# Softmax probabilities transposed in 32x32 blocks on VectorE and reordered through DRAM, in an attention and router kernel

## The chip, the cores and the metric

The kernel runs on one core of one Trainium2 chip. The metric is the device time of one execution in microseconds (us). Before the change it is 1690.57 us, the median of 3 runs (1690.31 to 1691.97).

## What is computed

One transformer layer on x of 4 x 512 rows by 512 columns: attention with 32 query heads of 128 and 8 key and value heads, then a router layer over 64 experts. The part that matters here:

```python
h = _layernorm(x) * (1 + ca) + sa
q = (h @ Wq.T).reshape(bsz, q_len, 32, 128).transpose(0, 2, 1, 3)      # then rotary embedding
scores = jnp.einsum('bhqd,bhkd->bhqk', q, k) * scale
scores = jnp.where(causal, scores, -1e9)
attn = jax.nn.softmax(scores, axis=-1)
out = jnp.einsum('bhqk,bhkd->bhqd', attn, v)
x = x + ga * (out.transpose(0, 2, 1, 3).reshape(bsz, q_len, 4096) @ Wo.T)
```

The router layer (layer norm, logits, softmax, the 8 largest, a mix of expert biases) follows for each of 16 tiles of 128 rows.

## The kernel before

A step t handles one query head of one batch row; there are 128 steps (`ALL`). Four steps are a unit u, the four query heads that share one key and value head for one batch row; h = t mod 4 says which. Every product is taken in three passes over operands split in a rounded high part (`_hi`) and the rest (`_lo`), so a transposed probability tile is written twice, as `PT_hi` by ScalarE and as `PT_lo` by VectorE.

Each engine has its own program, written out by hand in `step(t)`, and works it off strictly in order; the engines meet at semaphores. What TensorE does in step t of the old kernel, in this order:

- `transpose_part(t, 0)` and `(t, 1)` (L394): the probabilities of step t, 128x128 tiles, into the banks ta and tb. With part 2 there are 10 tiles, the causal half of 512 x 512 (`CAUSAL` = 1280 columns on 128 partitions).
- `scores(t+1)` (L376), with `transpose_part(t, 2)` in its middle.
- `q_proj(t+3)` (L336), the query projection for three steps on.
- by h: `out_proj(u-1)` at h = 0 (L428, four tiles of 12 matmuls), `k_proj` at h = 1 (L347), `v_proj` at h = 2 (L357), `v_transpose` at h = 3 (L364).
- `values(t)` (L408), probabilities times v, 12 matmuls into the bank pv.

VectorE in step t: `split_part_lo` (L956), `mask_and_max(t+1)` in two halves (L941, L945), `o_split_lo(t-1)` (L962), `invert_sums(t+1)` (L951), `q_rope(t+3)` (L920 to L922), at h = 1 `k_rope` (L927 to L929), at h = 0 `v_split_lo` (L933) and the four `add_out` (L970). ScalarE: `split_part_hi` (L696), `o_split_hi(t-1)` (L700), at h = 2 `k_nope` (L664, L665) and `k_split` (L671), `q_split(t+2)` (L654), `exponentials(t+1)` (L683), `normalise(t+1)` (L690). GpSimd (POOL): `q_split` (L1274), `q_rope` (L1269), `k_rope` (L1278), `k_split` (L1282) and the low parts of the next weights (L1265). SyncE's queue (SP) carries the weight pieces, the rows of x and the results; it has nothing per step.

From step 117 on the router layer runs in the same steps (`ffn_...`), mostly on VectorE and GpSimd.

## Time and profile before

| | |
|---|---|
| median of 3 runs | 1690.57 us |
| the profiled execution | 1689.32 us |
| its span, first to last instruction | 1688.0 us |
| granted TensorE clock, mean | 0.992 |
| busy share of the span: PE, PEld, DVE, ACT, POOL | 98%, 83%, 70%, 60%, 38% |
| chain that ended last, by engine | PE 87%, DVE 7%, issue 3%, ACT 2%, DMA 1%, POOL 1% |
| DMA | 54.20 MB, mean 32 GB/s |

The table is read from the top down: PE busy for nearly the whole span says little by itself, since matmuls overlap; that the chain which ended last lies on PE for 87% says that PE's order of work sets the time. The shares are averages over a prologue of about 100 us, the 117 plain steps and the last steps with the router layer.

### The profile page before, as it was taken

The page shows a single profiled execution, that of the slowest core. Times are in us where ns is not written, and L with a number is a line of the kernel's source. Part 1 is how long each engine was busy: PE and PEld are TensorE (multiplying, and loading weights), DVE is VectorE, ACT ScalarE, POOL GpSimd, SP SyncE. Part 2 cuts the span into 40 slices and gives each one's busy share as a digit, 9 for nine tenths or more (in the row PEclk, how much of TensorE's full clock was granted, in tenths as well). Part 3 has the DMA queues.
Part 4 walks back from the last instruction along what each step waited for, and adds up shares of the span by engine and source line. Part 5 has one row for each costly group of instructions (what it writes and reads, how often), then busy time and mean ns, then how long its engine had stood idle before and what let it go on. Part 6 is the DMA issues. An engine that isn't in the chain of part 4 may idle for free.

```text
span 1688.0 us, 25563 instructions
## 1 busy us (share of the span) xinstructions
PE 1648.9 (98%) x8880; PEld 1401.1 (83%) x8880; DVE 1177.1 (70%) x3413; ACT 1011.1 (60%) x2522; POOL 644.8 (38%) x524
## 2 busy tenths in 40 slices
PE   8999999999999999999999999999999999999977
PEld 5688888888888888888888888888888888887754
DVE  6866667766666667766666667766666667778798
ACT  3366666766656666766656666756656666755441
POOL 2753243423333233423333233423333233455674
PEclk9999999999999999999999999999999999999998
DMA  8410000100000000100000000100000000211032
GB/s 306 158 44 13 1 26 14 26 1 13 26 14 13 1 26 14 26 1 14 26 13 13 1 26 14 26 1 13 26 13 14 1 26 13 65 25 51 26 82 74
DMA packets 48975, 54.20 MB, mean 32 GB/s; under 512 B 19456, under 2 KB 27904, under 8 KB 48848
## 3 DMA queue, kind: packets, MB, share of 16 engines
q1 hardware_dynamic: 48528, 52.47, 10.2%
q8 instruction: 71, 1.16, 0.3%
q14 instruction: 56, 0.46, 0.1%
q10 hardware_dynamic: 320, 0.11, 0.0%
HBM read 45.20 MB, written 7.37 MB: 31 GB/s over the span
## 4 chain that ended last, share of the span: by engine, by line
PE 87%; DVE 7%; issue 3%; ACT 2%; DMA 1%; POOL 1%; SPq 0%; DVEq 0%; ACTq 0%
PE bank_q L336 20%; PE bank_pv L408 14%; PE bank_s L376 13%; PE bank_pv L428 10%; PE bank_x L428 10%; PE bank_x L357 5%; PE bank_ta L394 5%; PE bank_x L347 5%; PE bank_tb L394 3%; PE bank_s L324 1%; DVE PT_lo L956 1%; PE bank_x L364 1%; DMA wmod<-in_wmod 1%; DVE neg_max L945 1%; ACT probs L683 1%
## 5 line engine op out<-in xcount | busy, mean ns | idle before, releaser
L696 ACT ACTIVATE PT_hi<-bank_ta 128x512 fp32r<-128x512 f32 (+1 forms) x256 | 126.6, 494 | 437.5 <-PE bank_ta L394 436.4
L1274 POOL TENSOR_TENSOR qT_lo<-rot_c,qT_hi 128x512 fp32r<-128x512 f32 x128 | 167.8, 1311 | 445.4 <-ACT qT_hi L654 445.4
L683 ACT ACTIVATE probs<-probs,neg_max 128x512 f32<-128x512 f32 (+3 forms) x512 | 283.7, 558 | 86.7 <-DVE neg_max L945 86.7
L956 DVE TENSOR_TENSOR PT_lo<-bank_ta,PT_hi 128x512 fp32r<-128x512 f32 (+1 forms) x256 | 143.1, 559 | 221.4 <-ACT PT_hi L696 217.3
L1269 POOL TENSOR_TENSOR rot_c<-rot_c,rot_s 128x512 f32<-128x512 f32 x128 | 165.6, 1294 | 262.3 <-DVE rot_s L922 262.2
L690 ACT ACTIVATE probs<-probs,row_inv 128x512 f32<-128x512 f32 (+3 forms) x512 | 245.1, 552 | 0.0
L941 DVE CUSTOM_DVE_ANT_0 probs<-bank_s,mask 128x512 f32<-128x512 f32 (+3 forms) x512 | 231.2, 488 | 0.0
L336 PE MATMUL bank_q<-hT_lo,wq_hi 128*128 128x512 f32 x512 | 208.4, 407 | 0.0
L336 PE MATMUL bank_q<-hT_hi,wq_hi 128*128 128x512 f32 x512 | 201.0, 392 | 0.0
L336 PE MATMUL bank_q<-hT_hi,wq_lo 128*128 128x512 f32 x512 | 199.4, 390 | 0.0
L376 PE MATMUL bank_s<-kT_lo,qT_hi 128*128 128x512 f32 (+3 forms) x512 | 179.4, 350 | 0.9 <-ACT wc_out L617 0.6
L408 PE MATMUL bank_pv<-PT_lo,v_hi 128*128 128x512 f32 (+3 forms) x512 | 168.4, 329 | 4.0 <-DVE OT_lo L962 4.0
L376 PE MATMUL bank_s<-kT_hi,qT_lo 128*128 128x512 f32 (+3 forms) x512 | 165.7, 324 | 0.0
L408 PE MATMUL bank_pv<-PT_hi,v_lo 128*128 128x512 f32 (+3 forms) x512 | 165.3, 323 | 0.0
L408 PE MATMUL bank_pv<-PT_hi,v_hi 128*128 128x512 f32 (+3 forms) x512 | 165.2, 323 | 0.0
L376 PE MATMUL bank_s<-kT_hi,qT_hi 128*128 128x512 f32 (+3 forms) x512 | 165.0, 322 | 0.0
L394 PE MATMUL bank_ta<-ident,probs 128*128 128x128 f32 x768 | 127.2, 273 | 5.2 <-DVE PT_lo L956 4.5
L970 DVE TENSOR_TENSOR y<-bank_x,y 128x512 f32<-128x512 f32 x62 | 42.9, 691 | 103.8 <-PE bank_x L428 103.8
L336 PEld LDWEIGHTS bank_q<-hT_hi,wq_hi 128*128 128x128 f32 x512 | 96.0, 188 | 22.4
L408 PEld LDWEIGHTS bank_pv<-PT_lo,v_hi 128*128 128x128 f32 x512 | 97.1, 190 | 16.7 <-DVE PT_lo L956 4.0
L336 PEld LDWEIGHTS bank_q<-hT_hi,wq_lo 128*128 128x128 f32 x512 | 96.7, 189 | 16.5
L336 PEld LDWEIGHTS bank_q<-hT_lo,wq_hi 128*128 128x128 f32 x512 | 96.6, 189 | 15.6
(196 smaller groups left out, 4083.2 us busy)
## 6 DMA issues: line engine op xcount, KB each, us to landing
stage<-in_wq SPq DMA_DIRECT2D x32, 256.0 KB, 2.6
stage<-in_wo SPq DMA_DIRECT2D x32, 256.0 KB, 2.6
wmod<-in_wmod SPq DMA_DIRECT2D x6, 1024.0 KB, 10.1
y<-in_x SPq DMA_DIRECT2D x4, 1024.0 KB, 12.2
stage<-in_x SPq DMA_DIRECT2D x16, 256.0 KB, 2.7
out_y<-h SPq DMA_DIRECT2D x16, 256.0 KB, 2.0
wup_in<-in_wup SPq DMA_DIRECT2D x4, 768.0 KB, 10.5
wc_scratch<-wc_out SPq DMA_DIRECT2D x16, 192.0 KB, 2.1
```

Of the source, the lines that this page charges most:

```text
L336: mm = pe.matmul(bank["q"][:], w[:, h, c, :], x[:, b * CH + c, :], start=(c == 0 and n == 0), stop=(c == CH - 1 and n == 2))
L376: mm = pe.matmul(score_bank[qt], q[:, qt * P:(qt + 1) * P], k[:, 0:(qt + 1) * P], start=(n == 0), stop=(n == 2))
L394: mm = pe.transpose(bank[name][:, o:o + P], row(t, qt)[:, kb * P:(kb + 1) * P], ident[:])
L408: mm = pe.matmul(bank["pv"][:, kb * P:SEQ], a[:, kb, :], p[:, KEY_OFFSET[kb]:KEY_OFFSET[kb] + (QT - kb) * P], start=(kb == 0 and n == 0), ...
L428: mm = pe.matmul(ps[:], o[:, h, j * P:(j + 1) * P], w[:, h, :], start=(h == 0 and n == 0 and not end), stop=(h == GROUP - 1 and n == 2))
L683: ins = act.activation(row(t, qt), row(t, qt), ACT.Exp, bias=neg_max[m][:, qt:qt + 1], scale=SCALE, accum_out=row_sum[m][:, qt:qt + 1])
L690: ins = act.activation(row(t, qt), row(t, qt), ACT.Copy, scale=row_inv[t % 2][:, qt:qt + 1])
L696: act.activation(PT[0][:, at:at + size], bank[T_PARTS[n][0]][:, 0:size], ACT.Copy).then_inc(act_t, 1)
L941: ins = dve.tensor_tensor_reduce(row(t, qt), score_bank[qt], mask[:, SEQ - (qt + 1) * P:], 1.0, LOWEST, ALU.add, ALU.max, row_max[m][:, qt ...
L956: dve.tensor_tensor(PT[1][:, at:at + size], bank[T_PARTS[n][0]][:, 0:size], PT[0][:, at:at + size].bitcast(F32), ALU.subtract).then_inc(dv ...
L1269: pool.tensor_tensor(rot_c[:], rot_c[:], rot_s[:], ALU.add).then_inc(pool_a, 1)
L1274: pool.tensor_tensor(lo[:], rot_c[:], hi[:].bitcast(F32), ALU.subtract).then_inc(pool_q, 1)
```

## The change

- Up to step 124 (`moved(t)`: t < `BY_PE` = 125) the probabilities are no longer transposed on TensorE. VectorE transposes them in 32x32 blocks into `blocks`, which takes the place of the second probability buffer (`transpose_blocks`, five instructions); SP stores `blocks` to DRAM as one DMA of 128 rows of 5 KB, 640 KB in all (`store_blocks`), and loads it back as four DMAs, each to 32 partitions in pieces of 1280 bytes (`load_transposed`), into `PT_raw`.
- `PT_raw` is the memory of `PT_lo`, of which there is one. So the load for step t waits until `values(t-1)` is done (`pe_pv`), and for the store.
- ScalarE makes `PT_hi` from `PT_raw` in two halves of 640 columns (`split_moved_hi`); VectorE makes the first half of `PT_lo` and GpSimd the second (`split_moved_lo`).
- `values(t-1)` runs in step t, between `scores(t+1)` and `q_proj(t+3)`. Its moving operand and its output are read and written in four runs instead of one; `o_split` puts the queries back in order.
- `out_proj` uses the banks ta and tb; its third tile waits for the first `add_out`, which VectorE now does after `transpose_blocks(t+1)`.
- On SP the weight pieces come between the load and the next store.

```diff
+SUB = 32
+SUBS = P // SUB
+BY_PE = ALL - 3
...
-        PT = [whole.take(f"PT_{p}", [P, CAUSAL], F32R) for p in ("hi", "lo")]
+        PT_hi = whole.take("PT_hi", [P, CAUSAL], F32R)
+
+        PT_raw = Region(whole.at).take("PT_raw", [P, CAUSAL])
+        PT = [PT_hi, whole.take("PT_lo", [P, CAUSAL], F32R)]
...
+        blocks_d = [nc.dram_tensor(f"blocks{i}", [P, CAUSAL], F32).ap() for i in range(2)]
...
+        blocks = probs[1]
+        blocks_v = blocks[:].rearrange("p (j s a) -> p s j a", j=SUBS, a=SUB)
...
+        def out_bank(u, j):
+            names = ("pv", "x") if u == UNITS - 1 else ("ta", "tb")
+            return bank[names[j % 2]]
+
         def row(t, qt):
-            return probs[t % 2][:, q_offset(qt):q_offset(qt + 1)]
+            return probs[(t - BY_PE) % 2 if t >= BY_PE else 0][:, q_offset(qt):q_offset(qt + 1)]
+
+        def moved(t):
+
+            return t < BY_PE
+
+        def queries(ap, t):
+            return ap.rearrange("p (i q a) -> p i q a", i=SUBS, a=SUB) if moved(t) else ap
+
+        def queries_in_order(ap, t):
...
             def values(t):
                 u, h = t // GROUP, t % GROUP
-                pe.wait_ge(dve_t, 3 * t + 3)
+                if moved(t):
+                    pe.wait_ge(dve_t, t + 1)
+                    pe.wait_ge(pool_t, t + 1)
+                else:
+                    pe.wait_ge(dve_e, part_event(t, 3))
                 if h == 0:
                     pe.wait_ge(dve_v, u + 1)
-                    if u > 0:
-                        pe.wait_ge(dve_y, QT * u)
-                else:
+                if t > 0:
                     pe.wait_ge(dve_o, t)
                 for kb in KEY_ORDER:
+                    at, size = KEY_OFFSET[kb], (QT - kb) * P
                     for n, (a, p) in enumerate(passes(v, PT)):
-                        mm = pe.matmul(bank["pv"][:, kb * P:SEQ], a[:, kb, :],
-                                       p[:, KEY_OFFSET[kb]:KEY_OFFSET[kb] + (QT - kb) * P],
+                        if moved(t):
+                            to = bank["pv"][:].rearrange("p (i k) -> p i k", i=SUBS)[:, :, kb * SUB:P]
+                            ps = p[:].rearrange("p (i k) -> p i k", i=SUBS)[:, :, at // SUBS:(at + size) // SUBS]
+                        else:
+                            to, ps = bank["pv"][:, kb * P:SEQ], p[:, at:at + size]
+                        mm = pe.matmul(to, a[:, kb, :], ps,
                                        start=(kb == 0 and n == 0), stop=(kb == KEY_ORDER[-1] and n == 2))
...
-                transpose_part(t, 0)
-                transpose_part(t, 1)
+                if not moved(t):
+                    transpose_part(t, 0)
+                    transpose_part(t, 1)
+                    if moved(t - 1):
+                        values(t - 1)
                 if has1:
                     if n is not None:
                         tile_waits((bias, n - 3), (wT_copy, n - 4), (mixed, n - 5))
                     scores(t + 1, QUERY_ORDER[:2])
-                    transpose_part(t, 2)
+                    if not moved(t):
+                        transpose_part(t, 2)
                     scores(t + 1, QUERY_ORDER[2:])
                 else:
                     transpose_part(t, 2)
+                if t == 0:
+                    pe.wait_ge(dve_h, BATCH * CH)
+                elif moved(t):
+                    values(t - 1)
...
+            def split_moved_hi(t):
+                act.wait_ge(d_tr[t % 2], 16 * SUBS * (t // 2 + 1))
+                for half in range(2):
+                    at = slice(half * CAUSAL // 2, (half + 1) * CAUSAL // 2)
+                    act.activation(PT[0][:, at], PT_raw[:, at], ACT.Copy).then_inc(act_t, 1)
...
-                split_part_hi(t, 0)
-                split_part_hi(t, 1)
+                if not moved(t):
+                    split_part_hi(t, 0)
+                    split_part_hi(t, 1)
                 if n is not None:
                     ffn_exp(n - 3)
                     ffn_h2T(n - 2, "q")
-                if t > 0:
+                if not moved(t):
                     o_split_hi(t - 1)
-                if h == 0:
-                    v_split_hi(u)
+                    split_part_hi(t, 2)
+                if has2 and t > 0:
+                    q_split(t + 2)
                 if more and h == 2:
                     k_nope(u + 1)
                 if more and h == 3:
                     v_raw(u + 1)
-                if has2 and t > 0:
-                    q_split(t + 2)
-                split_part_hi(t, 2)
                 if has1:
                     exponentials(t + 1, 0)
                 if more and h == 2:
                     k_split(u + 1)
+                if t > 0 and moved(t):
+                    o_split_hi(t - 1)
+                if h == 0:
+                    v_split_hi(u)
                 if has1:
                     exponentials(t + 1, 1)
                     normalise(t + 1, 0)
                     normalise(t + 1, 1)
+                if moved(t):
+                    split_moved_hi(t)
...
+            def transpose_blocks(t):
+                if t > 0:
+                    dve.wait_ge(d_tw[(t - 1) % 2], 16 * ((t - 1) // 2 + 1))
+                dve.wait_ge(act_norm, 2 * t + 1)
+                for qt in QUERY_ORDER:
+                    if qt == 1:
+                        dve.wait_ge(act_norm, 2 * t + 2)
+                    keys = row(t, qt).rearrange("p (k j b) -> p k j b", j=SUBS, b=SUB)
+                    whole_keys = min(qt + 1, 3)
+                    ins = dve.transpose(blocks_v[:, qt:qt + 3 * whole_keys - 2:3], keys[:, 0:whole_keys])
+                    if qt == 3:
+                        dve.transpose(blocks_v[:, KEY_OFFSET[3] // P], keys[:, 3])
+                ins.then_inc(dve_tp, 1)
...
+            def split_moved_lo(t):
+                at = slice(0, CAUSAL // 2)
+                dve.wait_ge(act_t, 2 * t + 1)
+                dve.tensor_tensor(PT[1][:, at], PT_raw[:, at], PT[0][:, at].bitcast(F32), ALU.subtract).then_inc(dve_t, 1)
...
-                short = h == 3 and has3
-                early = h == 0 or not has3
-                split_part_lo(t, 0)
-                if not short:
+                if not moved(t):
+                    split_part_lo(t, 0)
                     split_part_lo(t, 1)
                 if has1:
                     mask_and_max(t + 1, 0)
-                if short:
-                    split_part_lo(t, 1)
-                split_part_lo(t, 2)
-                if t > 0 and early:
+                if not moved(t):
+                    split_part_lo(t, 2)
                     o_split_lo(t - 1)
                 if n is not None:
                     ffn_norm(n - 1)
                 if has1:
                     mask_and_max(t + 1, 1)
-                if not early:
+                if has1:
+                    invert_sums(t + 1, 0)
+                if t > 0 and moved(t):
                     o_split_lo(t - 1)
                 if h == 0:
                     v_split_lo(u)
-                if has1:
-                    invert_sums(t + 1, 0)
                 if n is not None:
                     ffn_top(n - 3)
                 if has1:
                     invert_sums(t + 1, 1)
                 if has3:
                     q_rope(t + 3)
+                if moved(t):
+                    split_moved_lo(t)
+                if moved(t + 1):
+                    transpose_blocks(t + 1)
...
+            def split_moved_lo(t):
+                at = slice(CAUSAL // 2, CAUSAL)
+                pool.wait_ge(act_t, 2 * t + 2)
+                pool.tensor_tensor(PT[1][:, at], PT_raw[:, at], PT[0][:, at].bitcast(F32),
+                                   ALU.subtract).then_inc(pool_t, 1)
...
+                if has3:
+                    q_rope(t + 3)
+                if moved(t):
+                    split_moved_lo(t)
+                if more and h == 1:
+                    k_rope(u + 1)
                 g, k = divmod(t - 1, STEPS)
                 for i in CHUNK_STEP.get(k + 1, []):
                     if not late(t) or i < 4:
                         split_piece(CHUNKS[i], i % 2, chunk_event(g, i))
-                if has3:
-                    q_rope(t + 3)
-                if more and h == 1:
-                    k_rope(u + 1)
                 if n is not None:
...
+            def store_blocks(t):
+                sp.wait_ge(dve_tp, t + 1)
+                if t >= 2:
+                    sp.wait_ge(d_tr[t % 2], 16 * SUBS * (t // 2))
+                sp.dma_start(blocks_d[t % 2], blocks[:]).then_inc(d_tw[t % 2], 16)
+
+            def load_transposed(t):
+                sp.wait_ge(d_tw[t % 2], 16 * (t // 2 + 1))
+                if t > 0:
+                    sp.wait_ge(pe_pv, t)
+                rows = blocks_d[t % 2].rearrange("(i b) (j x) -> j b i x", b=SUB, j=SUBS)
+                for j in range(SUBS):
+                    to = PT_raw[j * SUB:(j + 1) * SUB, :].rearrange("p (i x) -> p i x", i=SUBS)
+                    sp.dma_start(to, rows[j]).then_inc(d_tr[t % 2], 16)
...
+            load_chunk(0, 0)
+            load_chunk(0, 1)
+            store_blocks(0)
+            for t in range(ALL):
+                if moved(t):
+                    load_transposed(t)
+                if t >= 2:
+                    load_next(t)
+                if moved(t + 1):
+                    store_blocks(t + 1)
```

## Rows read from the trace of the kernel before

**Rows 1.** The page, part 1: busy us of each engine.

```profile
PE 1648.9 (98%) x8880; PEld 1401.1 (83%) x8880; DVE 1177.1 (70%) x3413; ACT 1011.1 (60%) x2522; POOL 644.8 (38%) x524
```

**Rows 2.** Chain that ended last, one unit: start us, us, what.

```profile
516.64 0.44 PE bank_ta L394 x4
...
530.58 2.72 PE bank_x L428 x12
...
535.20 0.44 PE bank_ta L394 x4
...
536.08 1.24 PE bank_s L376 x6
...
537.53 0.64 PE bank_s L376 x6
538.17 2.83 PE bank_q L336 x12
541.00 2.72 PE bank_x L347 x12
543.72 1.90 PE bank_pv L408 x12
...
556.01 0.44 PE bank_ta L394 x4
...
564.15 0.44 PE bank_ta L394 x4
```

**Rows 3.** Instructions in order of time: softmax of one step on DVE and ACT.

```profile
518.96 0.69 DVE L941 CUSTOM_DVE_ANT_0 probs<-bank_s,mask 128x512 f32<-128x512 f32 x1
...
520.39 0.71 ACT L683 ACTIVATE probs<-probs,neg_max 128x512 f32<-128x512 f32 x1
...
521.61 0.19 ACT L683 ACTIVATION_READ_ACCUMULATOR probs<-probs,neg_max 128x1 f32 x1
...
522.35 0.51 ACT L683 ACTIVATE probs<-probs,neg_max 128x256 f32<-128x256 f32 x1 [0.56 <-DVE neg_max L945]
...
523.16 0.19 ACT L683 ACTIVATION_READ_ACCUMULATOR probs<-probs,neg_max 128x1 f32 x1
...
523.25 1.91 ACT L690 ACTIVATE probs<-probs,row_inv 128x512 f32<-128x512 f32 x4
```

**Rows 4.** Groups by line and form, 500 to 900 us: busy us, mean ns | idle.

```profile
L956 DVE TENSOR_TENSOR PT_lo<-bank_tb,PT_hi 128x512 fp32r<-128x512 f32 x35 | 23.9, 682 | 0.0
...
L941 DVE CUSTOM_DVE_ANT_0 probs<-bank_s,mask 128x384 f32<-128x384 f32 x35 | 19.4, 553 | 0.0
...
L941 DVE CUSTOM_DVE_ANT_0 probs<-bank_s,mask 128x128 f32<-128x128 f32 x34 | 9.7, 284 | 0.0
```

**Rows 5.** The same view on ScalarE and on GpSimd.

```profile
L664 ACT ACTIVATE kv_raw<-bank_x 32x512 f32<-32x512 f32 x9 | 5.3, 591 | 4.2 <-POOL kv_raw L1278 4.0
L1278 POOL TENSOR_TENSOR kv_raw<-kv_raw,kv_rot 128x512 f32<-128x512 f32 x9 | 11.6, 1291 | 3.3 <-DVE kv_rot L929 3.3
```

**Rows 6.** DMA issues: count, KB each, median us from issue to landing.

```profile
out_y<-h SPq DMA_DIRECT2D x16, 256.0 KB, 2.0
...
stage<-wc_scratch SPq DMA_DIRECT2D x8, 128.0 KB, 3.1
...
experts<-in_eb SPq DMA_DIRECT2D x1, 128.0 KB, 2.5
router<-in_rw SPq DMA_DIRECT2D x1, 128.0 KB, 2.3
```

**Rows 7.** One line's instructions on SP: duration ns min/median/max.

```profile
L1433 SPq DMA_DIRECT2D stage<-wc_scratch x8: 662/672/683, 30.9 to 1271.0; - x8
L1461 SPq DMA_DIRECT2D router<-in_rw x1: 587/587/587, 1469.2 to 1469.2; - x1
```

**Rows 8.** Stretches: us, PE, PEld, DVE, ACT, POOL busy, PEclk, DMA share, GB/s.

```profile
10.00:20.00 10.00, 9.02 (x33) 3.58 (x31) 7.38 (x11) 3.09 (x5) 0.00 (x0) 1.00 1.04 405
...
78.00:80.00 2.00, 0.11 (x1) 0.14 (x2) 1.74 (x2) 0.22 (x1) 2.00 (x1) 0.97 0.00 0
80.00:82.00 2.00, 2.00 (x8) 2.00 (x9) 1.73 (x3) 0.41 (x1) 2.00 (x3) 0.50 0.01 4
...
1556.00:1568.00 12.00, 11.47 (x64) 9.45 (x65) 11.36 (x37) 7.31 (x19) 11.60 (x12) 1.00 0.14 44
```

More of the change, by code:

```diff
@@ L238, in build @@
         d_w = [sem(f"d_w{i}") for i in range(2)]
+        d_tw = [sem(f"d_tw{i}") for i in range(2)]
+        d_tr = [sem(f"d_tr{i}") for i in range(2)]
         d_xin, d_router = sem("d_xin"), sem("d_router")
@@ L418, in out_proj @@
                 for j in tiles:
-                    ps = bank["pv" if j % 2 == 0 else "x"]
-                    if j == 1 and not end:
-                        pe.wait_ge(dve_v, u + 2)
-                    if j >= 2:
-                        pe.wait_ge(dve_y, QT * u + j)
+                    ps = out_bank(u, j)
+                    if u > 0 or j >= 2:
+                        pe.wait_ge(dve_y, QT * u + j - (0 if j >= 2 else 1))
                     if end:
@@ L936, in mask_and_max @@
                 m = t % 2
+                if half == 0 and 0 < t <= BY_PE:
+                    dve.wait_ge(dve_tp, t)
+                if half == 0 and t == BY_PE + 1:
+                    dve.wait_ge(d_tw[t % 2], 16 * (t // 2))
                 for qt in HALVES[half]:
@@ L1106, in step @@
                     mask_and_max(t + 1, 0)
-                if short:
-                    split_part_lo(t, 1)
-                split_part_lo(t, 2)
-                if t > 0 and early:
+                if not moved(t):
+                    split_part_lo(t, 2)
                     o_split_lo(t - 1)
@@ L1203, in vector_program @@
             dve.wait_ge(pool_h, BATCH * CH)
+            transpose_blocks(0)
             for t in range(ALL):
@@ L1509, in sync_program @@
                 sp.wait_ge(s, 16 * (COMBINED // 4))
[L1511 to L1520 removed]
+            load_chunk(0, 0)
[8 more added lines that the diff above has]
+                    store_blocks(t + 1)
+                if t == ALL - STEPS + GROUP:
+                    load_rows(0)
+                if t >= ALL - STEPS + GROUP:
+                    n = ffn_tile(t)
+                    if n is not None and t + 1 < ALL:
+                        store_out(n - 4)
+                    ffn_load(t - (ALL - STEPS + GROUP))
+                    if n is not None and t + 1 == ALL:
+                        store_out(n - 4)
             for n in range(TILES - GROUP - 1, TILES):
```

63 lines of the change are left out of this document (32 added, 31 removed).

## The prediction

> **What bounds the kernel now.** I read three views. First the busy shares [rows 1]: TensorE is busy for 98%, VectorE for 70%, ScalarE for 60%. Matmuls overlap, so that alone proves nothing. Second the chain that ended last, through one whole unit of four steps [rows 2]: from 516.64 to 564.15 us every piece is TensorE's, with no wait and no other engine in it. A unit takes 47.51 us: step h = 0 18.56 (516.64 to 535.20), h = 1 10.42 (to the end of the value product at 543.72 + 1.90), h = 2 10.39 (to 556.01), h = 3 8.14 (to 564.15). So in the plain steps, units 0 to 28, only TensorE counts, and the others have slack of which this kernel makes no use. Third the stretches [rows 8]: from step 117 on it is otherwise. In 1556 to 1568 us VectorE is busy for 11.36 of 12 us, GpSimd for 11.60; there VectorE's own order sets the time.
>
> **What the change takes from TensorE.** Ten transposes a step. Four take 0.44 us [rows 2], so ten take 1.10. If nothing else moved, a unit would fall by 4.4 to 43.1 us, and the kernel by 128 x 1.10 = 141 us. That is the whole gain there can be. The value product keeps its 12 matmuls and 1.90 us [rows 2]. That its operand and its output come in four runs is shown by no row; I cost it at nothing (the rows nearest to it, all contiguous, say nothing against), and at twice 1.90 us as the other end. What hides it is that it lies once in the chain below.
>
> **What it puts on the other engines, per step.** The prices:
> - Block transposes on VectorE: three keys' worth of 384 columns for query tile 3 and 128 more, then 384, 256 and 128 columns. No row shows a transpose on this engine. The nearest are VectorE's operations of the same widths: 0.553 us for 384 columns, 0.284 for 128, and 0.418 midway for 256 [rows 4]. Sum 2 x 0.553 + 2 x 0.284 + 0.418 = 2.09 us. Ends: half of that, 1.05, if a copy-like operation runs faster, and double, 4.18, if writing in runs of 32 halves the rate. I take 2.09, the price of every operation of this width in the trace.
> - High half on ScalarE: 640 columns, 0.72 (the 512-column exponential takes 0.71, the 512-column copy 0.59 [rows 3, 5]). Low half on VectorE: 0.682 for 512 columns [rows 4] and 128 more at the slope of the rows, 0.82. Low half on GpSimd: 1.291 x 1.25 = 1.61 [rows 5].
> - The store, 640 KB: a store of 256 KB lands 2.0 us after its issue [rows 6]. The 393 KB (thousand bytes) more take 0.97 us at 405 GB/s, what the queues reach when they are full [rows 8]. So 3.0 us.
> - The load, four DMAs of 160 KB: an issue with a pattern of several dimensions holds SP for 0.59 to 0.67 us [rows 7], so the fourth goes out 1.8 us after the first. A DMA of 128 KB lands 2.3 to 3.1 us after its issue, the 3.1 being the one that reads back what the kernel had stored [rows 6]. With 2.8, the last quarter lands at 4.6 us. Ends for the pair: 2.9 and 3.8 if the quarters overlap wholly, 4.0 and 6.0 if they follow each other or the store's data are not read at once.
>
> VectorE loses `split_part_lo` (0.68 twice and 0.42, 1.79 us) and gains 2.09 + 0.82: 1.1 us more a step. ScalarE loses about as much as it gains.
>
> **What lies on the path.** The price of an engine's work says little; the order does. There is one PT_lo, one `blocks`, and every engine works in order. That makes a ring through each step:
> load(t) lands, ScalarE splits (0.72), VectorE splits (0.82), then in its order `transpose_blocks(t+1)` (2.09), then the store (3.0), then load(t+1) (4.6). One lap is 11.23 us. In the steps h = 1, 2, 3 TensorE would have 9.3, 9.3 and 7.0 us of work, so the lap is longer than the step. It can't make use of the long step h = 0 either: the load waits for the value product of the step before it, and `add_out`, on which the third tile of `out_proj` waits, stands on VectorE behind `split_moved_lo(t)` and `transpose_blocks(t+1)`.
> A second ring needs no DMA at all: `mask_and_max(t+1)` starts only behind `transpose_blocks(t)` on VectorE, and `transpose_blocks(t+1)` needs its normalised rows. From mask to the end of normalising takes 6.2 us (518.96 to 523.25 + 1.91 [rows 3]); with 0.72, 0.82 and 2.09 behind it a lap is 9.8, with the 0.59 of `o_split_hi`, now between the two halves of the exponentials, 10.4.
>
> I lined up one unit with these durations, every engine in its order, and followed it back. The chain, from `scores` at h = 1 to the next unit's:
> 1. scores 1.88, values(t of h = 0) 1.90: 3.8 (scores as 1.24 + 0.64 [rows 2])
> 2. load 4.6; split and block transposes 0.72 + 0.82 + 2.09 = 3.63: 12.0
> 3. `k_rope`, 3 x 0.68 on VectorE, behind the transposes; GpSimd's add 1.29; `k_nope` 2 x 0.59: 16.5
> 4. ScalarE at h = 2: first exponentials 1.41 (520.39 to 521.80), `k_split` 0.59, `o_split_hi` 0.59, second exponentials 1.00 (522.35 to 523.35), normalise 1.91 [rows 3, 5]: 22.0
> 5. split and transposes 3.63: 25.7
> 6. two laps of store, load, split and transposes, 2 x 11.23: 48.1
> 7. first `add_out` 0.68, then two tiles of `out_proj`, 2 x 2.72 [rows 2]: 54.2
> 8. some 15 hand-overs between engines at about 0.05 us, 0.7: 54.9.
>
> So a unit takes 54.9 us instead of 47.5, 7.4 more; 29 units make 215 us. TensorE works for 43.1 of 54.9 us, in gaps of 3 to 4 us ahead of the value products at h = 3 and h = 0. In the last 11 steps, where VectorE is full, I take the same 1.85 us a step, 20 us (lower end 1.1 x 11 = 12, the added work alone). The prologue stays: its chain has no probabilities. Sum: 1688.0 + 235 = 1923 us of span, 1924.3 of execution (1.3 lies around the span), and as the profiled execution was 1.25 below the median, 1925 as the time to expect.
>
> **A rule on the load.** The quarters go to 32 partitions each. In this trace the one DMA to 64 partitions, 128 KB, lands after 2.5 us, the one to 128 partitions after 2.3 [rows 6]: 0.2 us apart. The Trainium skill (SBUF — State Buffer, "Door 1: The DMA port swizzle") says that a transfer to 32 or 64 partitions reaches 8 of the 16 ports and so gets half the rate. By that rule the four quarters pass one port group after another and, as an estimate, the load takes 5 to 6 us. The difference in the row has its sign. Without the rule the same case is the long end of my bounds for the load, and I hold it for the second most likely.
>
> **The rivals.**
> - Faster, TensorE stays the bound: the rings overlap with the long h = 0 step, or transfers are so short that all is hidden. Then the 141 us come: 1549. For it: VectorE, ScalarE and the DMA queues all have room in the busy shares [rows 1]. Against it: even with transfers at nothing, the second ring of 10.4 us stands against steps of 9.3, 9.3 and 7.0. It would need 7 us less in my chain to break even. Chance 0.08; no change 0.02.
> - A smaller loss, transfers wholly hidden or block transposes at half price. With free transfers the two laps are of 10.4 and the load in 2 gives way to `q_rope` (2.81 + 2.07 before the split): about 53.4 a unit, + 171 + 16, 1877. With transposes at 1.05 the chain loses 4 x 1.04: 50.7, + 93 + 12, 1795. Chance of a time between 1770 and 1860: 0.12.
> - Slower, long transfers: load 6.0 and store 4.0 add 3 x 1.4 + 2 x 1.0 = 6.2 a unit, 13.6 more than now: 1690 + 394 + 37 = 2121. It decides once the load takes over 5 us. Chance of 2000 to 2130: 0.17.
> - Slower, the clock: in 78 to 80 us TensorE does 0.11 us of work, and in 80 to 82 it is granted 0.50, its 1.2 GHz level instead of 2.4 [rows 8]. The gaps forecast here are as long, two a unit. If each takes 1.5 us of work from the chain, that is 3 a unit, 93 us: 2018. I think it mostly falls into waiting time: behind the value product the load waits for the store anyway. It is in the chance above.
> - Slower, block transposes at double price: 4 x 2.09 = 8.4 a unit, 2176. Chance 0.06.
>
> **How the numbers follow.** The chain with its prices within some 0.8 us each way (1860 to 2000) has 0.55, which with the others makes 1. The predicted time is 1925. The range 1790 to 2100 takes in half-price transposes at its low end and load 5.8 with store 3.9 at its high end; outside are faster and no change (0.10), and the longest cases (0.10). Forecast, and all cases but the first rival, are slower: chances faster 0.08, within 0.2% 0.02, slower 0.90; 0.2% or 3.4 us is about what a measurement of this kernel can tell from none.
>
> **What would show it.** The gap before `values` in the waits of TensorE, released by the low splits of VectorE and GpSimd, 3 to 4 us at h = 3 and h = 0; some 2 us before the third tile of `out_proj`, released by `add_out`; `transpose` groups at 0.55 us for 384 columns; load and store medians of 4.6 (issue of the first to landing of the last) and 3.0; TensorE busy for about 80%; a clock below 1 behind the gaps. Step sizes of about 22 to 24, 9 to 10, 11 and 11 us for h = 0 to 3. It is wrong if the chain that ended last is still TensorE's alone, if the load lands in under 3 us, or if VectorE's transposes aren't near 2.1 us a step.

## The result and the profile after

The changed kernel takes 2018.3 us (median of 4 runs, 2017.0 to 2023.4), the kernel before beside it 1691.2. The ratio is 1.194, with a 95% interval of 1.192 to 1.196. The forecast was 1925 in a range of 1790 to 2100: sign and range held, the loss was 93 us larger than forecast.

The page of the profile after: its part 1 (busy us, share of the span), the granted clock in 40 slices (in tenths), and the shares of the chain that ended last.

```profile
span 2015.7 us, 24495 instructions
...
PE 1691.4 (84%) x7630; PEld 1399.1 (69%) x7630; DVE 1409.9 (70%) x3788; ACT 1021.0 (51%) x2397; POOL 890.4 (44%) x649
...
PEclk9989988988999988889898888898988888988897
...
PE 46%; DVE 15%; DMA 12%; ACT 11%; issue 10%; SPq 3%; POOL 2%; DVEq 0%; ACTq 0%; POOLq 0%
```

TensorE had 98% of a span of 1688.0 [rows 1]; it now has 84% of 2015.7, and not even fewer microseconds: it lost ten transposes a step and got slower matmuls. VectorE's share stays at 70%. No engine is full, and yet the kernel is 19% slower; only the chain tells why. Through one plain unit it reads (start us, us, what):

```profile
570.83 1.85 PE bank_s L412 x12
572.68 1.97 PE bank_pv L454 x12
...
597.21 2.89 DMA blocks<-probs
...
600.12 0.33 SPq L1563
...
601.43 3.80 DMA PT_raw<-blocks
...
605.26 0.75 ACT PT_hi L754
...
606.03 0.84 DVE PT_lo L1044
606.86 1.49 issue
608.36 3.18 PE bank_pv L454 x12
...
611.60 0.30 SPq L1563
...
613.25 3.65 DMA PT_raw<-blocks
...
616.93 0.75 ACT PT_hi L754
...
618.94 0.57 DVE probs L1036
...
620.68 0.59 DVE y L1057
...
621.30 3.03 PE bank_ta L471 x12
...
627.06 1.85 PE bank_s L412 x12
```

Where [rows 2] had only TensorE, the chain now leaves it. The first lap here goes through store, load, high half and low half; then it turns into the value product, and the second load goes out behind that product (608.36 + 3.18, then 611.60), not behind a store. From one `scores` to the same one of the next unit it is 56.2 us; this is one of the shorter units, and its chain is closer to the forecast than most. In 12 of the 26 units from 228 to 1729 us (units 2 to 27) the chain holds no store at all, in 13 one, and in one the two that were forecast. Of a unit of 59.2 us, the same view:

```profile
829.46 0.33 SPq L1563
...
830.79 3.79 DMA PT_raw<-blocks
...
834.61 0.75 ACT PT_hi L754
...
835.38 1.76 DVE PT_lo L1044
837.14 1.49 issue
838.63 3.88 PE bank_pv L454 x12
...
842.57 0.30 SPq L1563
```

That is a second kind of lap: load, high half, low half, the rest of GpSimd's half (the 1.49 us called issue), value product, and the next load. It takes 13.1 us here, 829.46 to 842.57, and has neither block transposes nor store in it. What SP waited for ahead of its loads from 400 to 1600 us (us in total, times, longest; the long waits for the value product behind `out_proj` are among the first), and what the third tile of `out_proj` waited for:

```profile
SPq L1559 <- PE bank_pv L454: 377.2, 84, 9.9
...
SPq L1563 <- DMA blocks<-probs: 35.0, 32, 3.2
```

```profile
PE bank_ta L471 <- DVE y L1057: 6.1, 5, 1.9
```

The whole loss adds up. From the first value product to the one 29 units on it is 1379.1 us before (104.3 to 1483.4) and 1675.1 after (112.4 to 1787.5): 47.55 and 57.76 a unit, 10.2 more, 296 in all. The first addition of the last stretch (step 117) starts at 1496.2 us before and at 1805.2 after, so 309.0 of the 327.7 us of span are lost by then: the 296, 8 ahead of the first value product (which now stands a step later) and 5 behind the 29 units. The other 18.7 come after it.

Now the price of the added operations, as lines of the page (busy us, mean ns | idle before, releaser), and of the DMAs (KB, us to landing):

```profile
L1367 POOL TENSOR_TENSOR PT_lo<-PT_raw,PT_hi 128x640 fp32r<-128x640 f32 x125 | 239.9, 1919 | 19.1 <-ACT PT_hi L754 18.3
...
L1044 DVE TENSOR_TENSOR PT_lo<-PT_raw,PT_hi 128x640 fp32r<-128x640 f32 x125 | 166.1, 1328 | 66.7 <-ACT PT_hi L754 65.8
...
blocks<-probs SPq DMA_DIRECT2D x125, 640.0 KB, 2.9
PT_raw<-blocks SPq DMA_DIRECT2D x500, 160.0 KB, 3.1
stage<-in_wq SPq DMA_DIRECT2D x32, 256.0 KB, 3.6
```

The store is as forecast (3.0) by its median. Both low halves are not: 1.33 instead of 0.82 on VectorE, 1.92 instead of 1.61 on GpSimd. In the instructions in order of time, VectorE's low half (L1044) appears at two prices in this stretch (start us, us, engine, line, idle before); the first three lines are VectorE's, the other four GpSimd's:

```profile
606.03 0.83 DVE L1044 TENSOR_TENSOR PT_lo<-PT_raw,PT_hi 128x640 fp32r<-128x640 f32 x1 [1.56 <-ACT PT_hi L754]
...
617.70 1.32 DVE L1044 TENSOR_TENSOR PT_lo<-PT_raw,PT_hi 128x640 fp32r<-128x640 f32 x1 [0.74 <-ACT PT_hi L754]
618.94 0.57 DVE L1036 STREAM_TRANSPOSE probs<-probs 128x384 f32<-128x384 f32 x1
```

```profile
604.54 1.26 POOL L1357 TENSOR_TENSOR rot_c<-rot_c,rot_s 128x512 f32<-128x512 f32 x1 [5.13 <-DVE rot_s L986]
606.70 1.56 POOL L1367 TENSOR_TENSOR PT_lo<-PT_raw,PT_hi 128x640 fp32r<-128x640 f32 x1 [0.89 <-ACT PT_hi L754]
...
617.04 1.29 POOL L1357 TENSOR_TENSOR rot_c<-rot_c,rot_s 128x512 f32<-128x512 f32 x1 [6.31 <-DVE rot_s L986]
618.37 2.07 POOL L1367 TENSOR_TENSOR PT_lo<-PT_raw,PT_hi 128x640 fp32r<-128x640 f32 x1
```

At 606.03 GpSimd has been idle since 605.80, and VectorE takes 0.83. At 617.70 GpSimd is in the middle of `q_rope`'s addition, until 618.33; VectorE's operation ends 0.69 after that, at 619.02. GpSimd's own half, due at 618.33, takes 2.07 and ends 1.42 after VectorE's. So each waits for the other's operation to end and then takes roughly its own time. The block transpose at 618.94 runs beside the same GpSimd operation and stays at 0.57. The Trainium skill (SBUF — State Buffer, "Who interferes with whom") says it of exactly such a pair: a VectorE instruction with two SBUF inputs contends with a GpSimd instruction that reads SBUF, and one with at most one SBUF input, outside VectorE's two-port modes, does not. The trace agrees, 0.83 against 1.32 and no change for the transpose. The kernel before had no such meeting in this split: its low half read one operand from PSUM (`bank_tb`) [rows 4]; the changed one reads `PT_raw` and `PT_hi`, both in SBUF.

### The profile page after: what moved, and what is told of

Same layout as the page of the kernel before. It is cut to its first block, busy times and chain, and to the rows that moved or that the text cites. A ratio compares the mean times of both kernels' runs of the same rounds, so it can differ in the third digit from the quotient of the medians.

```text
span 2015.7 us, 24495 instructions
## 1 busy us (share of the span) xinstructions
PE 1691.4 (84%) x7630; PEld 1399.1 (69%) x7630; DVE 1409.9 (70%) x3788; ACT 1021.0 (51%) x2397; POOL 890.4 (44%) x649
## 4 chain that ended last, share of the span: by engine, by line
PE 46%; DVE 15%; DMA 12%; ACT 11%; issue 10%; SPq 3%; POOL 2%; DVEq 0%; ACTq 0%; POOLq 0%
PE bank_pv L454 12%; PE bank_q L372 9%; DMA PT_raw<-blocks 8%; PE bank_ta L471 7%; PE bank_tb L471 7%; PE bank_s L412 5%; DVE probs L1036 4%; PE bank_x L383 3%; DMA blocks<-probs 3%; DVE PT_lo L1044 3%; ACT probs L733 3%; SPq L1563 3%; ACT PT_hi L754 3%; ACT probs L740 2%; POOL kv_raw L1372 2%
## 5 line engine op out<-in xcount | busy, mean ns | idle before, releaser
L454 PE MATMUL bank_pv<-PT_lo,v_hi 128*128 128x512 f32 (+3 forms) x512 | 214.5, 419 | 250.8 <-issue 241.8
L1367 POOL TENSOR_TENSOR PT_lo<-PT_raw,PT_hi 128x640 fp32r<-128x640 f32 x125 | 239.9, 1919 | 19.1 <-ACT PT_hi L754 18.3
L754 ACT ACTIVATE PT_hi<-PT_raw 128x640 fp32r<-128x640 f32 x250 | 170.6, 730 | 148.3 <-DMA PT_raw<-blocks 148.3
L1044 DVE TENSOR_TENSOR PT_lo<-PT_raw,PT_hi 128x640 fp32r<-128x640 f32 x125 | 166.1, 1328 | 66.7 <-ACT PT_hi L754 65.8
L1036 DVE STREAM_TRANSPOSE probs<-probs 128x384 f32<-128x384 f32 x500 | 202.4, 442 | 2.1 <-POOL hT_lo L1347 2.1
L454 PE MATMUL bank_pv<-PT_hi,v_hi 128*128 128x512 f32 (+3 forms) x512 | 203.6, 398 | 0.0
L454 PE MATMUL bank_pv<-PT_hi,v_lo 128*128 128x512 f32 (+3 forms) x512 | 203.4, 397 | 0.0
L984 DVE TENSOR_TENSOR rot_c<-bank_q,cos_t 128x512 f32<-128x512 f32 x128 | 88.4, 691 | 123.6 <-PE bank_q L372 121.4
L1049 DVE TENSOR_TENSOR OT_lo<-bank_pv,OT_hi 128x512 fp32r<-128x512 f32 x128 | 88.4, 690 | 89.3 <-ACT OT_hi L758 89.3
L412 PEld LDWEIGHTS bank_s<-kT_lo,qT_hi 128*128 128x128 f32 x512 | 98.1, 192 | 53.3 <-issue 40.9
## 6 DMA issues: line engine op xcount, KB each, us to landing
wmod<-in_wmod SPq DMA_DIRECT2D x6, 1024.0 KB, 10.2
```

The source lines that it names most:

```text
L412: mm = pe.matmul(score_bank[qt], q[:, qt * P:(qt + 1) * P], k[:, 0:(qt + 1) * P], start=(n == 0), stop=(n == 2))
L454: mm = pe.matmul(to, a[:, kb, :], ps, start=(kb == 0 and n == 0), stop=(kb == KEY_ORDER[-1] and n == 2))
L754: act.activation(PT[0][:, at], PT_raw[:, at], ACT.Copy).then_inc(act_t, 1)
L1036: ins = dve.transpose(blocks_v[:, qt:qt + 3 * whole_keys - 2:3], keys[:, 0:whole_keys])
L1044: dve.tensor_tensor(PT[1][:, at], PT_raw[:, at], PT[0][:, at].bitcast(F32), ALU.subtract).then_inc(dve_t, 1)
L1367: pool.tensor_tensor(PT[1][:, at], PT_raw[:, at], PT[0][:, at].bitcast(F32), ALU.subtract).then_inc(pool_t, 1)
```

## The experiments

All ratios are against the kernel before, run beside each on the same chip (1690 to 1692 us).

**1. No transfers.** Stores and loads are left out, the splits read `PT_lo` in place, so the probabilities' data are not computed. Every other instruction of the steps stays; one memset ahead of them fills `PT_lo`.

```
-                act.wait_ge(d_tr[t % 2], 16 * SUBS * (t // 2 + 1))
+                act.wait_ge(dve_tp, t + 1)
+                act.wait_ge(pe_pv, t)
...
-                if moved(t):
-                    load_transposed(t)
...
-                if moved(t + 1):
-                    store_blocks(t + 1)
```

> This kernel stores and loads nothing per step: the splits start from what lies in PT_lo, once the block transposes of the step and the value product before it are done, so the probabilities that reach the value product are not the right ones; all instructions of the engines stay. Theory of the rings (every engine's order makes loops through split, block transposes, mask and normalise; transfers are one term of them): in my bookkeeping the unit falls from 58 us to about 55, since the ring without transfers (about 11 us a lap with the splits as slow as they are now) takes over; 29 units of 3 us, about 1920 us, 1880 to 1950. Rival, transfers are the cause (with them gone TensorE is the bound again): 1550 to 1690 us. Rival, transfers are hidden: within 10 us of 2018.

1917.8 us, ratio 1.134 (1.132 to 1.136), clock 0.932. With free transfers 100 us of the 327 go and 227 stay: for the faster rival more than 327 had to go. So two thirds of the loss stay with no transfer at all. That they are the rings through VectorE is the reading of this, and its chain fits it only in part: TensorE has 52% there, VectorE 23%.

**2. Quarters over all partitions.** The same four DMAs of 160 KB, each to 128 partitions x 320 columns instead of 32 x 1280; the data arrive in the wrong places.

```
-                    to = PT_raw[j * SUB:(j + 1) * SUB, :].rearrange("p (i x) -> p i x", i=SUBS)
-                    sp.dma_start(to, rows[j]).then_inc(d_tr[t % 2], 16)
+                    x = slice(j * CAUSAL // SUBS, (j + 1) * CAUSAL // SUBS)
+                    sp.dma_start(PT_raw[:, x], blocks_d[t % 2][:, x]).then_inc(d_tr[t % 2], 16)
```

> The load is still four DMAs of 160 KB in pieces of 1280 bytes, but each goes to all 128 partitions, a quarter of the columns (so the blocks are not put in their places). If the ports that 32 partitions reach are what makes the last quarter land 5.1 us after the first issue instead of 4.6, it lands at about 4.3 and the kernel falls by 3 x 0.8 us a unit, to about 1950 us. If the issues on SP and the fixed latency make it, the landing stays at 5.0 to 5.2 and the time within 10 us of 2018.

2012.2 us, ratio 1.189 (1.184 to 1.193), whose interval overlaps that of the changed kernel (1.192 to 1.196), so the 6 us are hardly told from none. A miss in time, not in the load: the median quarter lands after 2.6 us instead of 3.1, and the load at 603.61 us is in by 607.91, 4.3 instead of 5.1. The gain is eaten one link further (its chain):

```profile
604.93 2.99 DMA PT_raw<-blocks
...
607.94 0.74 ACT PT_hi L754
...
608.71 0.03 DVE PT_lo L1044
...
608.99 1.38 issue
610.37 0.57 DVE probs L1036
```

From 608.71 to 610.37 VectorE is in its low half, 1.66 us instead of 0.84 at 606.03 in the changed kernel: its median over the kernel rises from 1.375 to 1.417, since it now comes more often into GpSimd's addition.

**3. One load.** One DMA of 640 KB, 128 rows, in place of the four; data in the wrong places again.

```
-                for j in range(SUBS):
...
-                    sp.dma_start(to, rows[j]).then_inc(d_tr[t % 2], 16)
+                sp.dma_start(PT_raw[:], blocks_d[t % 2]).then_inc(d_tr[t % 2], 16)
```

> One DMA of 128 rows of 5 KB instead of four (the blocks are not put in their places). It should land about 3.0 us after its issue, as the store of the same size does (2.9), 2.1 us sooner than the last quarter now. Theory of the rings: three loads lie in the chain of a unit, but the ring without transfers takes over after some 3 us, so about 1920 us, near the kernel without any transfers. If each load's time counts in full (three a unit): 2018 - 29 x 6.3 = 1835. If the load is hidden: 2018.

1931.1 us, ratio 1.142 (1.140 to 1.144). The load lands after 3.8 us, the clock is 0.927. It is nearly as good as no transfers at all (1918), for a reason that shows in the durations (min/median/max ns) of VectorE's low half and of GpSimd's addition:

```profile
L1044 DVE TENSOR_TENSOR PT_lo<-PT_raw,PT_hi x125: 824/826/1845, 108.8 to 1829.7; 128x640 fp32r<-128x640 f32 x125
...
L1357 POOL TENSOR_TENSOR rot_c<-rot_c,rot_s x128: 1262/1908/1942, 69.7 to 1829.7; 128x512 f32<-128x512 f32 x128
```

In the changed kernel the medians are 1375 and 1287. The data are now there when VectorE gets to its low half at h = 0 and 1, so it starts 0.02 to 0.05 us ahead of GpSimd's addition, and GpSimd waits; at h = 2 VectorE still waits (1.76 us on average). The same happens in experiment 1 (median 826). So a faster load looks like a step: next to nothing as long as VectorE comes second (experiment 2), most of it once it comes first. That is argued from these two runs; nothing between them was tried.

**4. GpSimd's half behind VectorE's.** One wait ahead of line 1367.

```
                 pool.wait_ge(act_t, 2 * t + 2)
+                pool.wait_ge(dve_t, t + 1)
```

> GpSimd begins its half of the low part only after VectorE's half is done, so the two never read and write SBUF together there. If the 1.37 us of VectorE's half and the 2.10 of GpSimd's (against 0.83 and 1.54 where they do not meet in the trace) come from their meeting, VectorE's half goes back to 0.83 in every step and GpSimd's to 1.55; the block transposes start 0.5 us sooner, the GpSimd half ends about 0.2 us later at most; four such terms lie in the chain of a unit: 2018 - 29 x 2 = about 1960, 1930 to 1990. If the slowness is of the form itself (640 columns from SBUF), the durations stay at 1.37 and 2.10 and the time rises by up to 40 us.

2029.7 us, ratio 1.200 (1.198 to 1.202), 11 us slower than the changed kernel: a miss. GpSimd's half falls to a median of 1.541, VectorE's stays at 1.340. The two halves were not what VectorE met; it was `q_rope`'s addition, which this leaves in place.

**5. Block transposes ahead of the low half.**

```
+                if moved(t + 1):
+                    transpose_blocks(t + 1)
                 if moved(t):
                     split_moved_lo(t)
-                if moved(t + 1):
-                    transpose_blocks(t + 1)
```

> Only the order on VectorE changes: the block transposes of step t+1 come before the low half of step t, so the landing of a load and the splits behind it no longer stand before the next store. Theory of the rings: that takes load, high half and low half out of the lap; in the bookkeeping with the measured prices the unit falls from 58.4 to 54.1 us, 29 x 4.3 = 125 us: about 1893, 1860 to 1930. Rival (the value product's wait on the single PT_lo is what counts, whatever VectorE's order): within 15 us of 2018.

2007.3 us, ratio 1.188 (1.184 to 1.191): a miss again. The ring of transfers is gone, only 1% of its chain is DMA, and VectorE has 38%:

```profile
606.57 2.00 DVE PT_lo L1044
...
608.62 3.89 PE bank_pv L454 x12
612.51 3.55 PE bank_q L372 x12
```

GpSimd's half runs from 606.35 to 607.89, and now VectorE's waits for that (median 1.843); and TensorE goes idle ahead of the value product, which with `q_proj` is in the chain at the lower clock. The chain was broken in the place that I attacked and closed again on VectorE.

**6. GpSimd's half ahead of its `q_rope`, and behind VectorE's half.** Nothing of `q_rope` can then run beside VectorE's low half.

```
                 pool.wait_ge(act_t, 2 * t + 2)
+                pool.wait_ge(dve_t, t + 1)
...
+                if moved(t):
+                    split_moved_lo(t)
                 if has3:
                     q_rope(t + 3)
-                if moved(t):
-                    split_moved_lo(t)
```

> GpSimd does its half of the low part before the rotary sum of the queries, and only after VectorE's half: VectorE's half now meets no operation of GpSimd. If meeting any SBUF operation of GpSimd is what holds VectorE's half (1.37 us in the kernel, 1.39 in the run where only the two halves were kept apart and the rotary sum still met it), it falls to 0.83 now and GpSimd's half to 1.55: in the bookkeeping 56.3 us a unit instead of 58.4, about 1955, 1930 to 1990, if the later rotary sum costs nothing. If the half is slow for another reason it stays at 1.37 and the time at 2018 or above.

1956.3 us, ratio 1.157 (1.155 to 1.159), as expected. Both halves at their own price, with hardly any spread:

```profile
L1044 DVE TENSOR_TENSOR PT_lo<-PT_raw,PT_hi x125: 824/825/828, 109.9 to 1865.1; 128x640 fp32r<-128x640 f32 x125
...
L1368 POOL TENSOR_TENSOR PT_lo<-PT_raw,PT_hi x125: 1533/1541/1582, 110.8 to 1866.0; 128x640 fp32r<-128x640 f32 x125
```

The transfers are as they were (2.9 and 3.1), so these 62 us are the meeting of the two engines and what follows from the new order. The two are not apart: the value product starts 0.1 us behind GpSimd's half at h = 1, 2 and 3 in both kernels, and that half no longer stands behind `q_rope`'s addition. What the low half holds VectorE for before the block transposes falls by 2.1 us a unit (four steps, 1.27 to 0.74 each), and the unit by 1.8 (57.76 to 55.95), so the meeting on VectorE alone would be enough for it.

**7. Both orders**, 5 and 6 without the wait.

> VectorE's block transposes before its low half, as in the run with the transposes first, and GpSimd's half before its rotary sum and as soon as its half of PT_hi is there. In the run with the transposes first, VectorE's half rose to 1.84 us, since GpSimd's half had begun before it; here GpSimd should be through both its operations by then, and the half be back at 0.83. If that collision and not the order is why that run gained only 11 us, the bookkeeping gives 51.9 us a unit, 4 less than with 1.84: 2007 - 29 x 4 = 1890, and 1830 if the slow clock behind the shorter waits goes too. If the order itself doesn't pay, about 1955, as in the run with GpSimd's split first.

1962.1 us, ratio 1.160 (1.157 to 1.164): not the 1890 of the collision, but the 1955 of an order that doesn't pay. VectorE's half is at a median of 1.455, so the collision was not removed, and what the order alone is worth this run doesn't tell; behind the transposes it falls onto GpSimd's operations wherever these stand. Chain: TensorE 43%, VectorE 33%, DMA 3%.

**8. Keep the clock.** Twelve matmuls whose result nobody uses, ahead of the value products of h = 0 and 3, in the plain steps.

```
+            def keep_busy(u, h):
+                pe.wait_ge(dve_y, QT * (u if h == 3 else u - 1) + 1)
+                for _ in range(12):
+                    pe.matmul(bank["tb"][:], hT[0][:, 0, 0:P], hT[0][:, 0, :], start=True, stop=True)
...
                 elif moved(t):
+                    if h in (0, 3) and 4 <= t < 112:
+                        keep_busy(u, h)
                     values(t - 1)
```

> Twelve matmuls of no use, 2.7 us at full clock, are put before the value product at h = 0 and h = 3, where TensorE waits 3.2 to 4.1 us; their result is not used. The granted clock should rise from 0.90 to 0.97 or more and the value product at h = 0 and 3 go from 3.2 us back to 1.95. If the slow clock falls into time in which the load waits for the store anyway, as the prediction had it, the kernel gains 0 to 30 us (1990 to 2018). If it stands in the chain in full: 2 x 1.3 us a unit, 75 us, about 1943.

1988.5 us, ratio 1.176 (1.172 to 1.181), 30 us faster, with more work done. The granted clock from 400 to 1600 us goes from 0.89 to 0.98. Not all of the 30 need be the clock: VectorE's low half also falls to a median of 1.108. And the forecast chain comes back. Of units 2 to 27, 20 have two stores or more in it and 21 the `add_out` (1 and 6 in the changed kernel). Of the 52 loads at h = 3 and h = 0 in them, 5 go out within 0.2 us of the end of a value product, where it was 37.

**9. Block transposes twice**, each step's again behind the first ones, with a wait between.

```
+                ins.then_inc(dve_z, 1)
+                dve.wait_ge(dve_z, t + 1)
+                for qt in QUERY_ORDER:
...
+                    ins = dve.transpose(blocks_v[:, qt:qt + 3 * whole_keys - 2:3], keys[:, 0:whole_keys])
```

> The block transposes are done twice in a row, with the same result: 1.95 us more on VectorE a step. Theory of the rings: four of them lie in the chain of a unit, 7.6 to 8 us a unit, 29 units, plus the last steps: 2018 + 230 = about 2250, 2220 to 2290. If VectorE's work were covered by waits for transfers, the time would hardly move (under 2050); if every one counted, 125 x 1.95 = 244, 2262, which is not told apart from the theory.

2237.1 us, ratio 1.323 (1.321 to 1.326): 219 us more than the changed kernel. The durations of the five transposes sum to 2.03 us, but each starts before the one ahead of it ends, and the second set starts 1.77 us behind the first:

```profile
709.67 0.56 DVE L1037 STREAM_TRANSPOSE probs<-probs 128x384 f32<-128x384 f32 x1
...
711.44 0.58 DVE L1045 STREAM_TRANSPOSE probs<-probs 128x384 f32<-128x384 f32 x1
```

125 x 1.77 = 221 us of added time, so nearly all of it counts. Stores have 8% of the chain here instead of 3, so it goes over them more often than in the changed kernel.

**10. `add_out` first.** Experiment 7, and the first of the four additions of `add_out(u-1)` ahead of the transposes at h = 0.

```
+                if h == 0 and t > 0 and not end(u):
+                    add_out(u - 1, [0])
                 if moved(t + 1):
                     transpose_blocks(t + 1)
```

> As the run with both orders, and the first add_out of a unit before the block transposes, so that the third tile of out_proj waits no longer: 0.8 to 1 us a unit less in the bookkeeping, 25 us less than that run. If out_proj's third tile is not in the chain any more, the same within 5 us.

1940.2 us, ratio 1.146 (1.143 to 1.148): 22 us less than experiment 7. The wait of `out_proj`'s third tile for VectorE's order was real there: 17 waits, 12.5 us in all from 400 to 1600 us in experiment 7, none here.

**11. The same with experiment 8's matmuls.**

> The same, with the twelve matmuls of no use before the value product at h = 0 and h = 3. With load and store out of VectorE's lap, the value product and the query projection behind it stand in the chain (they took 3.3 to 3.9 and 3.2 to 3.6 us at the lower clock in the run with the transposes first, against 1.9 and 2.8), so the clock should be worth more here than the 30 us it was worth in the kernel itself: 40 to 90 us less than without them. If it is worth 30 or less, the clock is not what the reordered kernel waits for. The floor of all these versions is the ring of mask, exponentials, normalising and block transposes, so none should come under 1750.

1873.8 us, ratio 1.108 (1.106 to 1.109): 66 us less, with a clock of 1.00 from 400 to 1600 us. The same matmuls gave 30 where DMAs and SP's issues are 15% of the chain and VectorE 15%, and 66 where TensorE has 50% of it and DMAs and issues 4%. This is the fastest version here, still 11% slower than the kernel before.

**12. Experiment 10 without transfers**, with the edit of experiment 1 (data not computed).

> The kernel with both orders changed and the first add_out first (1940 us), now without its stores and loads, as in the first run without transfers (the probabilities that reach the value product are not the right ones). If the reordering has taken the transfers off the chain, as its chain says (DMA 3% against 12% in the kernel), the time stays within 25 us of 1940, where the same removal was worth 100 us in the kernel itself. What then bounds it is the ring of value product, query projection, rotary products, block transposes and low half, with no transfer in it. If the transfers still count, it falls by 60 us or more, towards 1870.

1909.5 us, ratio 1.129 (1.127 to 1.131): transfers are worth 31 us here (25 at most was expected), and 100 in the kernel as changed. With neither transfers nor the old order its chain has 50% of TensorE and 33% of VectorE.

## Why the prediction was right, and where it was short

**What bounds.** Right in part. TensorE is no longer the bound, a ring through the single `PT_raw` and the in-order queues is, and the start of the unit is as forecast, in its order and its sizes. In the unit shown, counted from its start at 570.83: end of the first block transposes 12.4 (forecast 12.0 at the end of part 2), `k_nope` 17.0 (16.5, part 3), end of normalising 22.3 (22.0, part 4), next transposes 26.4 (25.7, part 5), the next unit 56.2 (54.9). Step sizes were 9.3, 11.7, 10.4 and 24.8, then 9.3, 11.3, 12.4 and 23.3, for forecasts of 9 to 10, 11, 11 and 22 to 24. Over units 2 to 27 the steps are 24.2, 9.3, 11.4 and 12.9 us for h = 0 to 3: the step at h = 3 is 1.9 longer than forecast.

**The laps: not the ones named.** I had both laps at the end of the unit go through block transposes and store, since "behind the value product the load waits for the store anyway". In the changed kernel 37 of the 52 loads at h = 3 and h = 0 of units 2 to 27 go out within 0.2 us of the end of a value product. I never priced that lap. At my own prices it was 9.6 us (load 4.6, two high halves 1.44, GpSimd's half 1.61, value product 1.90), under the 11.2 of the other, and so it was right to leave it out at those prices; as measured it is 13.1 in the lines from 829.46, with 1.76 + 1.49 behind the first high half and 3.88 for the value product at the lower clock. The wait for `add_out` that closed my chain is in it in 6 units of 26; in the others it ends in value product, `q_proj` and four tiles of `out_proj`. So the time came out within 5% partly by luck: other links took the place of those named and were about as long.

**The added operations.** Block transposes right one by one, by the groups by form from 600 to 1000 us: 0.549, 0.400 and 0.266 us for 384, 256 and 128 columns, in blocks of 32 as fast as any other operation of that width. Their sum, 2.03 a step for a forecast of 2.09, is not what the chain pays: from the start of the first to the end of the last it is 1.74 us (581.51 to 583.25 in the view shown), as their records overlap. So I charged 0.35 a step too much, 1.4 a unit, and that hid part of what I had too low. The value product in four runs takes 1.97 us for 1.90 at full clock, so nothing was the right price for it. Store 2.9 for 3.0, high half 0.75 for 0.72: right.

**VectorE's low half: a term mis-sized.** I took the slope of rows whose operand lay in PSUM and got 0.82. Its own price is that, 0.825 (experiment 6), but in the kernel it is 1.33 on average, as both operands now lie in SBUF; that is read from the trace, and no run put the operand back in PSUM. The same on GpSimd: 1.54 alone for a forecast of 1.61, 1.92 in place. Experiment 6 prices the meeting, with the order on GpSimd that it changes too, at 62 us. No term and no rival of the prediction had it.

**The load.** Forecast 4.6. The two in the lines shown take 5.1 and 5.3 (600.12 to 605.23, 611.60 to 616.90); the mean over steps 8 to 111, first issue to last landing, is 4.85, under the point (over 5) from which the rival of long transfers was to decide. At three loads a unit the 0.25 would be 0.75 us, 22 us in all, an estimate from the ring as forecast. The rule of the Trainium skill on 32 partitions (SBUF — State Buffer, "Door 1: The DMA port swizzle") has the right sign, but the time to landing is not halved: over 128 partitions a quarter lands after 2.6 us instead of 3.1. The kernel gains 6 us by it at most (experiment 2), as the rest goes into the meeting in the lines shown. Experiment 3 is worth 87 us, together with the order in which the engines meet; how much of it is the load alone these runs don't separate.

**The clock.** The forecast was "mostly into waiting time", and 93 us for the rival. The measured 30 lies between; that the rival's own time, 2018, is the measured one is chance. Stretches of 2 us of the kernel after (columns as in [rows 8]) show the gap, the drop behind it and a value product in it:

```profile
606.00:608.00 2.00, 0.00 (x0) 0.00 (x0) 1.97 (x5) 1.66 (x3) 1.30 (x1) 1.00 0.03 6
608.00:610.00 2.00, 1.64 (x6) 1.54 (x7) 1.92 (x9) 0.00 (x0) 2.00 (x3) 0.79 0.34 141
610.00:612.00 2.00, 2.00 (x9) 1.90 (x9) 1.49 (x7) 1.21 (x3) 0.74 (x1) 0.50 0.49 195
```

TensorE does nothing for 4.1 us up to 608.36; once it works again its grant falls, to 0.79 in the next stretch and to 0.50, its 1.2 GHz level, in the one after, and the value product takes 3.18 us instead of 1.97 (3.88 in the longer lap). It ends at 611.54, and the load goes out behind it at 611.60. So the clock reached the ring through the very wait that I had set down as its cover. Experiment 8 is the test: with the clock at 0.98 the loads wait for the store again.

**The sum.** The 29 plain units cost 296 us instead of 215 (57.8 instead of 54.9 each), 81 of the miss. The last stretch costs 18.7 instead of 20, 1 less. The 13 us ahead of and behind the plain units had no term; the cause of these was not tried apart. Together 93. The two largest parts priced by a run, 62 and 30 us, overlap and do not add, since experiment 8 also changed how the engines meet; that their sum is near 93 proves nothing.

**The rivals.** Free transfers were to give 1877 and gave 1918 (experiment 1); what made the 41 was not tried apart. Transposes at double price were to add 251 (2176 for 1925) and added 219, on a base that is 93 higher; at 1.77 us a set instead of 2.09 they would have been to add about 212. The faster rival falls with experiment 1; its 141 us count 128 steps, and 125 are changed, so 138 was all there could be.

Left open: a second `PT_raw`, with which load(t+1) would not have to wait for value product t. It wasn't tried.

## What to carry to other kernels

Taking work from the full engine is worth nothing if the result goes in a ring through one buffer and several in-order queues: write down the lap of every ring through that buffer (here 11 us by one way and 10 by the other, 13 as it ran) beside the shortest step (7 us) before the busy shares. Two rings of nearly the same length change places when one term grows, and a term that was covered (here the clock) then counts. When an operand moves from PSUM to SBUF, ask which GpSimd operation can run beside its reader on VectorE; here a new order of two calls on GpSimd, with a wait, gave back 62 of 327 us. Breaking one ring gave 11 us where the next one was as long (experiment 5): count the second ring first.

## What was unexpected of the hardware

- Who waits is decided by who starts first: VectorE's low half takes 0.825 us alone, 1.33 on average and up to 1.89 us in the kernel; with an earlier load (experiment 3) it is GpSimd's addition that goes from 1.29 to 1.91.
- A tiny operation can pay as much, and with one SBUF operand only: the scaling of two columns, `neg_max` (L1013), takes 0.17 us alone and 1.00 at 598.44, beside GpSimd's subtraction (598.13 to 599.41). VectorE's operations that read PSUM stay at 0.69 beside GpSimd (597.23) and the block transposes at 0.57 (618.94).
- Loads of weights of 256 KB land after 3.6 us where they took 2.6 before, beside 218 MB of traffic instead of 54.
- One DMA of 640 KB that writes DRAM lands after 2.9 us, one of the same size that reads it back after 3.8.
